# Dummy transposes on TensorE between the first products and the first scores of a two-layer transformer kernel

## What is computed

```
xn = layernorm(x)
x = x + attention0(xn) + mx_linear(xn)        # layer 0
    # attention0: differential attention, 16 heads, each with two score maps of
    #   head size 4; o = softmax(q1 k1) v - lam * softmax(q2 k2) v, then rms norm, projection
    # mx_linear: both operands rounded to a 6-bit grid in blocks of 32
xn = layernorm(x)
x = x + attention1(xn) + binary_mlp(xn)       # layer 1
    # attention1: 16 heads of size 8 with rotary embedding, softmax, projection
    # binary_mlp: three products with weights of -1 and 1, relu between (256-512-512-128)
```

## Time and profile before

| what | value |
|---|---|
| median of 3 executions | 922.26 us (919.93 to 922.6) |
| the profiled execution, its own time | 924.88 us |
| its span from the first to the last instruction | 922.8 us |
| TensorE busy | 842.5 us, 91% |
| ScalarE busy | 776.0 us, 84% |
| VectorE busy | 551.6 us, 60% |
| GpSimd busy | 24.4 us, 3% |
| mean granted clock of TensorE | 0.969 |

### The profile page before, as it was taken

How to read it: one execution, slowest core, us unless ns; L and a number is a source line. 1 busy time by engine, 2 the same in 40 slices (tenths; PEclk the granted TensorE clock), 3 DMA queues, 4 the chain that set the end, 5 groups by cost and what they waited for, 6 DMA issues and landing times. The chain is left out here.

```text
span 922.8 us, 18566 instructions
## 1 busy us (share of the span) xinstructions
PE 842.5 (91%) x7005; PEld 312.0 (34%) x7005; DVE 551.6 (60%) x1340; ACT 776.0 (84%) x866; POOL 24.4 (3%) x37
## 2 busy tenths in 40 slices
PE   5288888899999999999999999999999899999996
PEld 4022222244343333333343333333333323333342
DVE  6176467675767466856767466856668456366221
ACT  1297988678988998899989998899988879888884
POOL 1000000000000000000000000000000000000000
PEclk9599999899999999999999999999999989999998
DMA  7905205423335307180245307170154504206000
GB/s 205 157 2 138 44 11 153 139 32 53 112 87 138 52 2 198 46 143 3 89 110 137 54 1 196 50 137 7 67 132 120 70 2 139 50 1 195 4 12 12
DMA packets 30453, 76.12 MB, mean 82 GB/s; under 512 B 6240, under 2 KB 8160, under 8 KB 27152
## 3 DMA queue, kind: packets, MB, share of 16 engines
q1 hardware_dynamic: 28972, 71.00, 33.1%
q10 hardware_dynamic: 748, 1.77, 0.8%
q0 software_dynamic: 640, 2.10, 0.7%
HBM read 37.37 MB, written 35.65 MB: 79 GB/s over the span
## 5 line engine op out<-in xcount | busy, mean ns | idle before, releaser
L644 ACT ACTIVATE probs<-ps_s 128x1024 f32<-128x1024 f32 x768 | 733.4, 1036 | 103.3 <-PE ps_s L798 100.3
L817 PE MATMUL ps_pv<-probs,v_aug 128*32 128x512 f32 x3072 | 416.5, 614 | 8.6 <-DVE pv_sb L1182 4.3
L798 PE MATMUL ps_s<-q_ab,k_ab 18*128 18x512 f32 (+1 forms) x1088 | 144.6, 504 | 39.8 <-DMA k_ab<-parts_dram 21.8
L798 PEld LDWEIGHTS ps_s<-q_ab,k_ab 18*128 18x128 f32 (+1 forms) x1088 | 55.0, 185 | 178.0 <-ACT probs L644 120.9
L817 PEld LDWEIGHTS ps_pv<-probs,v_aug 128*32 128x32 f32 x3072 | 61.9, 109 | 120.6 <-issue 79.9
L669 PE MATMUL ps_misc<-h_hi,k_w 128*128 128x512 f32 x192 | 86.3, 449 | 3.0 <-ACT ff_out L609 1.3
L798 PE MATMUL ps_s<-q_c,k_c 34*128 34x512 f32 x448 | 82.3, 445 | 0.0
L670 PE MATMUL ps_misc<-h_lo,k_w 128*128 128x512 f32 x192 | 75.6, 394 | 0.0
L1023 DVE CAST h_hi<-ff_out 128x512 fp32r<-128x512 f32 x64 | 27.4, 428 | 79.2 <-ACT ff_out L609 76.9
L1182 DVE COPY pv_sb<-ps_pv 128x512 f32<-128x512 f32 x48 | 33.2, 692 | 67.5 <-PE ps_pv L817 64.9
L669 PEld LDWEIGHTS ps_misc<-h_hi,k_w 128*128 128x128 f32 x192 | 35.9, 187 | 89.9 <-issue 41.1
(11 more groups left out here) (136 smaller groups left out, 588.9 us busy)
## 6 DMA issues: line engine op xcount, KB each, us to landing
parts_dram<-qk_parts SPq DMA_DIRECT2D x47, 512.0 KB, 3.1
q_ab<-parts_dram SPq DMA_DIRECT2D x64, 128.0 KB, 4.7
k_ab<-parts_dram SPq DMA_DIRECT2D x60, 128.0 KB, 6.5
parts_dram<-qk_parts SPq DMA_DIRECT2D x30, 256.0 KB, 3.5
q_c<-parts_dram SPq DMA_DIRECT2D x14, 512.0 KB, 7.0
k_c<-parts_dram SPq DMA_DIRECT2D x14, 512.0 KB, 8.9
x_all<-in_L_attn_x_dram SPq DMA_DIRECT2D x8, 256.0 KB, 13.6
out_dram<-x_all POOLq DMA_DIRECT2D x8, 256.0 KB, 6.6
```

Of the source, the lines that this page charges most:

```text
L644: nc.scalar.activation(probs[:, U.slot(s), 2 * half:2 * half + 2], ps_s[:, 2 * pair:2 * pair + 2], ACT.Exp, scale=SCALE[U.layer]).then_inc ...
L798: ins = nc.tensor.matmul(ps_s[:, bank, :], k[row:row + n, slot, c * P:(c + 1) * P], q[row:row + n, slot, :], start=True, stop=True)
L817: ins = nc.tensor.matmul(ps_pv[32 * j:32 * j + 32, :], v_aug[:, U.v, c, a:a + 32], probs[:, U.slot(s), j, :], start=c == 0 and not odd, st ...
```

## The change

TensorE gets 200 more dummy transposes, of the same form as the 60 at the start. `warm(n)` writes n of them. 50 stand behind the prologue's flag and branch, 40 behind a wait for the write of q's parts, and 110 behind a wait for the write of k's parts. Then come the old wait for the ones in k and the first unit. The 60 at the start are the same as before. Nothing is changed on another engine.

```diff
-WARM = 60
+
+WARM, WARM_WAITS = 60, (50, 40, 110)
...
+            def warm(n):
+                for _ in range(n):
+                    nc.tensor.transpose(ps_s[:, 0, 0:P], ident[:], ident[:])
+
             pe.wait_ge(pool_made, 2)
-            for _ in range(WARM):
-                nc.tensor.transpose(ps_s[:, 0, 0:P], ident[:], ident[:])
+            warm(WARM)
             run(PROLOGUE[:-1])
             exact_max(0, 0, heads_within(0, 0))
+            warm(WARM_WAITS[0])
+            for i in range(2):
+                pe.wait_ge(parts_written[0][i], WRITTEN[i])
+                warm(WARM_WAITS[1 + i])
             pe.wait_ge(k_ones_loaded, K_ONES)
```

## The result

The changed kernel takes 928.75 us (median of 6 runs, 926.19 to 930.48) against 921.92 us (918.63 to 925.73) of the kernel before beside it: ratio 1.0075, 95% interval 1.0053 to 1.0098, so 5 to 9 us slower and most likely 6.9. The forecast was slower by 4.4 us, 926.7, with a range of 920.5 to 931.5. The direction and the range held; the size came out more than half as large again. The likeliest case's own range, 925.7 to 928.1, did not hold: 928.75 lies in the stated range only by what had been added for late code and for the clock's later falls, so the range was hit with some luck.

What follows compares the result with a forecast made beforehand. Start bound by q and k over DRAM until 38.96 us, then TensorE at 1.2 GHz, then ScalarE. First scores +6.0 us, less the warm clock's gain, taken as +4.4: 922.26 to 926.7 us, range 920.5 to 931.5.

Steps and rivals of the forecast that it cites:

- likeliest case: Dummies overrun k's landing and delay the first scores: 926.7 us, own range 925.7 to 928.1; chance 0.60.
- late code: Rival at the start: instruction packets for the 200 transposes arrive late and TensorE stands, 928 to 933 us; chance 0.08.
- the clock's later falls: Rival behind the start: four later clock falls turn out fewer or more, 923.3 to 930.1; chance 0.17 of within 0.3% or below.
- Where the dummies start: On TensorE behind the prologue's flag, written at 19.06, not behind the products at 16.80: start at 21.0 us.
- What they cost: Dummies: 21 cold at 0.213 us over 4.5 us, then 179 warm at 0.109, ending at 45.0 us.
- The waits: TensorE's waits for q's and k's writes, done by 19.74 and 23.82, hold nothing; all 200 dummies run in one piece.
- What is late next: First scores +6.0 us, to 45.0; first exponential 45.5; step 5 +4.0; VectorE's chain +4.7, at 53.0; taken as +4.4.
- That nothing behind swallows the delay: Behind the start no wait ends at a fixed time, so the delay goes through to the end.
- the gain of the warm clock: First unit's steps 0 to 4 at 1.83 us give 1.76 us, the first exponential 0.3 sooner: together 2.1 us.
- The cover: TensorE's idle time up to 38.96 us hides 18 us of the 24 us of dummies; the rest lies open.
- The dummies end in time: Rival at the start: dummies leave the queue by 38.96, gain of 1.3 to 2.1 us, 920.2 to 921.0; chance 0.12.
- The transposes stay cold: Rival: all 200 dummies run at half clock and end at 63.6, +24.6 us, 946.9; chance 0.03.

Runs made afterwards that it cites:

- experiment with the waits alone: The change's two waits kept, no dummies behind the products, against the kernel before: 922.81 us against 920.81, ratio 1.0017.
- 250 dummies: The change with 250 dummies (50, 40, 160) instead of 200, against the kernel before: 932.4 us, ratio 1.0116.
- the late cold start: No dummies behind the products, the two waits kept, TensorE waits for all tokens before the first scores; against the kernel before 931.71 us, ratio 1.0106.
- the held clock: 140 dummies instead of 200, plus 9, 9 and 3 in steps 0 to 2 of the first unit: ratio 1.0007; the same on the change's 200: 1.0064.
- the last three kernels: Lambda exponential before the first unit, tokens' wait later, weight transpose at step 2: no dummies 0.9981; with 9, 9, 3 in steps 0-2 and 140 0.9952, 115 0.9956.
- the early chain: Lambda exponential ahead of the first unit, VectorE's tokens' wait behind its quantisation, weight transpose at step 2, no dummies behind the products: 919.61 us against 921.92, ratio 0.9981.
- The kernel with both but the transpose still at step 7: Lambda exponential and tokens' wait moved, weight transpose at step 7, 140 dummies plus 9, 9 and 3 in steps 0 to 2: 919.65 us, ratio 0.9980.

## Why the prediction was right, and where it was too small

**Where the dummies start** was forecast as 21.0 and is 20.76, behind the flag's load, as read from VectorE's row. **What they cost**: 25 of them ran at half clock for about 5.4 us (421 ns each, as in the earlier trace rows) and 175 at full clock; I had taken 4.5 us and 21. They end at 45.42 instead of 45.0. One of the two rises behind that 4.5 was misread: TensorE had been busy without a gap not since 45.4 but since 42.78, 6.5 us before the clock rose at 49.3:

```profile
42.78 0.80 PE L798 MATMUL ps_s<-q_ab,k_ab 18*128 18x512 f32 x4 [1.11 <-ACT probs L644]
```

The bounds of 3.4 and 6.8 still take in both rises, and the 5.4 measured. **The waits** cost nothing measurable (experiment with the waits alone). **What is late next**: first scores at 45.35 against 45.0, first exponential at 45.89 against 45.5, VectorE's chain released at 53.59 against 53.0. Every one of these is within 0.6 us. (That a transfer of k lands 15 us after its issue, in the rival on late code, is misread: 15 us is from the first issue to the first scores, and one transfer took 6.0 to 13.7.) **That nothing behind swallows the delay** holds in the main: with 250 dummies and with the late cold start, 10.7 of 11.2 and 9.8 of 12.6 us arrive at the end.

**The term that failed is the gain of the warm clock.** I had put it at 2.1 us; it took the delay of 6.0 down to 4.0 at ScalarE's step 5 and to 4.7 at VectorE's chain, and to 4.4 in the sum. The sum assumed "steps of 1.83" for steps 0 to 4 because the clock would be full when they begin. The exponentials of these steps took 1.8, 1.8, 2.0, 2.6 and 2.6 us, together 10.8 against 10.9 before, and with step 5 it is 13.4 us against 12.7: a loss of 0.7. Step 5 started 6.0 us later than before and not 4.0. The clock was full when the steps began, and fell between the third and the fourth scores, since TensorE was busy for less than half of the first steps; filled with dummies it did not fall. The rows showed this: before, too, TensorE waited for ScalarE in steps 0 and 1, 0.80 us of work in 1.91. I asked what the clock would be at the first scores and not what those scores would do to it. Without the credit the sum is +6.0, plus 0.4 for the longer dummies, and the measured one is +6.9. The cover was a single execution's as well: the idle time up to 38.96 hid 18 us of dummies, but the operands were complete at 37.2 in the changed kernel's profile. What the cover is on average no run shows, so the agreement of 6.4 with 6.9 must not be pressed.

And even the held clock does not earn those 2.1 us: with steps 0 to 5 in 11.0 us the kernel with 140 dummies is at 1.0007, and the change at 1.0064. In the prediction I had VectorE's chain in the sum, but only as a second shift of +4.7. It is a limit of its own: in no profile with the chain in its old place does the copy come sooner than 11.4 us behind ScalarE's line 649, and TensorE waits for it. In the change it took longer still, 66.92 - 53.59 = 13.3 us, for VectorE in its turn stood 2.10 us for TensorE's transpose of the weight, late from the 10 us at half clock (0.28 before). So the copy came 7.1 us late and not 4.7. That both limits have to go together is borne out by the last three kernels: 0.9981 with the early chain, 1.0007 with the held clock, 0.9952 and 0.9956 with both. The kernel with both but the transpose still at step 7 measured 0.9980, as without the held clock, though its first unit was shorter; that is not explained.

**The rivals.** "The dummies end in time" was tried twice, by count and by place, and gives 1.0003 and 1.0027, not the forecast gain; but in both profiles the dummies still ended 1.9 and 2.3 us behind the operands. They ended in time, by 0.3 us, with 115 dummies and once with 140, where k landed late (39.7), and both of these kernels also had VectorE's early chain. So the rival's price, 1.3 to 2.1 us of gain, has no clean test; what is shown is that the warm steps it rests on don't come without something to hold the clock. "The clock's later falls move" is real: second, third and 20th units differ by 1.3 to 3 us from profile to profile. In the changed kernel's profile they return about 4 us: the second unit starts 9.8 us late, the last units 5.8, and the span is 5.0 us longer. "The transposes stay cold" is out: 176 transposes ran with a granted clock of 1.00. The Trainium skill, page "TensorE: Matmul & The Clock Gate", section "Part 4: PE-mode transpose", says the contrary; these fp32 transposes raised the clock and kept it, and the measurement decides. "Code comes late" is out too: the 200 dummies have no gap among them.

What stays open: the 200 dummies ahead of the flag measure 0.27% slower than before and the 140 behind it nothing, while in their profiles both overran their operands by about the same, 2.3 and 1.9 us. The intervals, 0.07% to 0.46% and -0.18% to 0.24%, overlap, so they need not differ. The two waits measured 0.17%, with an interval that reaches nothing; I would not build on either. What sets the place of the later falls was not tried.

## What to carry to other kernels

Work that keeps a clock warm is free only as long as it ends before the wait it fills; what runs beyond that delays everything behind it, for it stands on the queue of the very engine that is needed next. Here 0.8 to 1.0 of such a delay arrived at the end. Size it from the row of the load's landing less the row in which it can really start (here 18 us and not the idle 21.8), and leave a margin, since the landing moved from 35.7 to 39.7 us between profiles: 140 dummies, sized by one profile, were 1.0 to 1.9 us late in three of four, and 115 ended 0.3 us ahead.

A warm clock at the first real instruction is worth something only if the work behind it is dense enough to keep it and if no other engine is the limit there. Look at the busy share of the first steps before counting the gain, and ask which engine is next.

## What the runs showed of the hardware that I had not expected

The clock fell about 4.6 us after the dense dummies gave way to steps in which TensorE was busy for 1.71 of 4.10 us (3.0 us after with 140 dummies, 4.25 with 200 ahead of the flag), and no gap in them was longer than 1.32 us. It then stayed at half for 10 us although TensorE was busy for 9.87 of the 10.10. Before, it had come back 6.5 us after the last gap (42.78 to 49.3), at the very start after 3.4 us of dummies, and with the dummies behind the flag after 5.4. So a fall can cost longer than the last rise suggests.

The register load of the flag (VectorE stands 2.04 us for it) costs TensorE nothing when matmuls are already queued ahead of it: with the dummies ahead of the flag the scores follow them at once, at 39.11.

A higher mean clock is not a faster kernel: the median over the runs is 0.974 before, 0.983 with the change, which is slower, and 0.983 with 140 dummies, which is as fast as before. Before, 20.3 us at half clock lay where TensorE had nothing to do, and there a full clock buys nothing. Among the runs of one kernel it does go with the time: of 23 runs of the kernel before, the fastest (917.45 us) had 0.979 and one of the slowest (924.91) had 0.968.
